# Prefetching streamed K blocks ahead of the output store, and a low-rank FFN loop skewed by five instead of four

## The reference, cut to what matters

```python
x = L0_attn_x                                   # (4, 8192, 1024) float32
q = x @ Wq;  k = x @ Wk;  v = x @ Wv            # 1024 x 1024 each
s = q @ k^T, causal, scaled by 1/32
x = layernorm(x + softmax(s) @ v @ Wo)
P = x @ U1                                      # 1024 -> 256
H = gelu(P @ V1 + b1)                           # 256 -> 4096
Q = H @ U2                                      # 4096 -> 256
x = layernorm(x + Q @ V2 + b2)                  # 256 -> 1024
```

## Time and profile before

| | us |
|---|---|
| median of 2 runs | 2522.15 (2521.6 to 2522.7) |
| profiled execution, its own time | 2539.7 |
| its span, slowest core (core 6) | 2538.2 |
| spans of its 8 cores | 2498.4 to 2538.2 |
| mean granted TensorE clock of its cores | 0.938 to 0.944 |

### The profile page before, as it was taken

How to read it: one execution, slowest core, us unless ns; L and a number is a source line. 1 busy time by engine, 2 the same in 40 slices (tenths; PEclk the granted TensorE clock), 3 DMA queues, 4 the chain that set the end, 5 groups by cost and what they waited for, 6 DMA issues and landing times.

```text
span 2538.2 us, 43250 instructions; the slowest of 8 cores (2498.4 to 2538.2 us)
## 1 busy us (share of the span) xinstructions
PE 2166.1 (85%) x14288; PEld 1353.6 (53%) x14288; DVE 770.8 (30%) x1882; ACT 665.7 (26%) x1389; POOL 353.0 (14%) x653
## 2 busy tenths in 40 slices
PE   0799899999677798788898989898979799897995
PEld 0354445555345465556565556565656566565663
DVE  0233334444235533432314141404040311303104
ACT  0000000000034344424334242424243332423323
POOL 3001111111310010110110202030202112021120
PEclk9999899999878898899898989898989899898997
DMA  9979998886361121132241616171717356182560
GB/s 125 143 99 150 142 135 164 168 163 146 104 105 42 55 84 46 59 134 82 85 152 49 216 49 218 67 233 37 255 59 257 110 171 220 59 293 82 184 223 17
DMA packets 219886, 328.79 MB, mean 130 GB/s; under 512 B 122688, under 2 KB 127824, under 8 KB 218656
## 3 DMA queue, kind: packets, MB, share of 16 engines
q0 software_dynamic: 51120, 166.84, 27.3%
q1 hardware_dynamic: 168560, 159.18, 23.2%
HBM read 287.92 MB, written 77.07 MB: 144 GB/s over the span
## 4 chain that ended last, share of the span: by engine, by line
PE 54%; DVE 7%; ACT 4%; issue 3%; DVEq 3%; POOL 1%; DMA 1%; ACTq 0%; POOLq 0%; SPq 0%
PE ps_s L499 16%; PE ps_a L524 9%; PE ps_a L526 8%; PE ps_x L614 5%; PE ps_a L627 4%; PE ps_a L565 2%; PE ps_s L565 2%; DVE x1t L782 1%; PE ps_s L627 1%; DVEq L807 1%; PE ps_a L499 1%; PE ps_x L549 1%; PE ps_s L646 1%; PE ps_s L549 1%; DVE x L808 1%
## 5 line engine op out<-in xcount | busy, mean ns | idle before, releaser
L663 ACT ACTIVATE p_sb<-ps_s,shift_s 128x256 bf16<-128x256 f32 x512 | 240.8, 473 | 696.1 <-PE ps_s L499 696.0
L499 PE MATMUL ps_s<-qg,kst 128*128 128x256 bf16 x2808 | 363.3, 272 | 3.6 <-DMA kst<-kscr 3.6
L403 POOL DMA_DIRECT2D vst<-vscr x351 | 188.0, 538 | 1131.7 <-PE ps_a L526 1045.6
L499 PEld LDWEIGHTS ps_s<-qg,kst 128*128 128x128 bf16 x2808 | 272.7, 97 | 112.3 <-issue 5.2
L252 PE MATMUL ps_s<-xt,wk_sb 128*128 128x512 bf16 x1024 | 228.9, 384 | 79.9 <-DMA wk_sb<-wk 50.1
L526 PE MATMUL ps_a<-vst,p_sb 128*128 128x512 bf16 x702 | 264.7, 377 | 0.0
L524 PE MATMUL ps_a<-vst,p_sb 128*128 128x512 bf16 x702 | 264.0, 376 | 0.0
L750 DVE RECIPROCAL recip<-ps_x 128x1 f32<-128x1 f32 x32 | 3.7, 158 | 771.4 <-PE ps_a L526 771.2
L663 ACT ACT_TABLE_LOAD x30 | 38.5, 1283 | 694.0 <-PE ps_a L499 693.8
L627 PE MATMUL ps_a<-p_sb,v_sb 128*128 128x256 bf16 x704 | 146.9, 310 | 85.2 <-DVE p_sb L824 85.2
L522 PE MATMUL ps_x<-ones_b,p_sb 128*128 128x1 bf16 x1088 | 180.4, 166 | 36.2 <-POOL p_sb L409 28.0
(11 more groups left out here) (109 smaller groups left out, 2517.5 us busy)
## 6 DMA issues: line engine op xcount, KB each, us to landing
vst<-vscr POOLq DMA_DIRECT2D x351, 256.0 KB, 4.6
kst<-kscr SPq DMA_DIRECT2D x351, 256.0 KB, 4.7
xbf<-x_seq POOLq DMA_DIRECT2D x16, 1024.0 KB, 14.6
xo<-x_own SPq DMA_DIRECT2D x32, 512.0 KB, 4.2
out<-outb SPq DMA_DIRECT2D x32, 512.0 KB, 3.2
kscr<-kstage POOLq DMA_DIRECT2D x51, 256.0 KB, 7.0
vscr<-vstage POOLq DMA_DIRECT2D x51, 256.0 KB, 3.5
xobf<-x_own POOLq DMA_DIRECT2D x16, 512.0 KB, 17.9
```

Of the source, the lines that this page charges most:

```text
L403: g.dma_start(out=vst[:, slot * 1024:(slot + 1) * 1024], in_=vscr_a[kb - R]).then_inc(vstS[slot], 16)
L499: mm = t.matmul(sbank(kb), k_tile(g_i, kb, dc), qg[:, qb + dc * 256:qb + (dc + 1) * 256], start=(dc == 0), stop=(dc == 7))
L663: sc.activation(p_sb[:, (it % 3) * 256:(it % 3 + 1) * 256], sbank(kb), AF.Exp, bias=shift_s[:, 0:1], scale=SCALE).then_inc(sem_exp, 1)
```

## The change

It has two parts. In SP's queue, `out_dma(g_i - 1)` moves from before the K loads of group `g_i` to behind them. In the FFN loop, `q2_partial` runs five slices behind `h` and no longer four, so that TensorE's order is h(0) to h(5), q2(0), h(6), q2(1), ..., h(31), q2(26), then q2(27) to q2(31). No instruction is added or dropped, and no wait is changed.

```diff
                 for g_i in range(NG):
-                    if g_i > 0:
-                        out_dma(g_i - 1)
                     for kb in range(R, 4 * g_i + 4):
                         si = SI[(g_i, kb)]
                         if si >= RING:
@@
                         slot = si % RING
                         s.dma_start(out=kst[:, slot * 1024:(slot + 1) * 1024],
                                     in_=kscr_a[kb - R]).then_inc(kstS[slot], 16)
+                    if g_i > 0:
+                        out_dma(g_i - 1)
                     gg = g_i + 2
@@
                         mm.then_inc(sem_h, 1)
-                        if fc >= 4:
-                            q2_partial(fc - 4)
-                    for fc in range(28, 32):
+                        if fc >= 5:
+                            q2_partial(fc - 5)
+                    for fc in range(27, 32):
                         q2_partial(fc)
```

## The result

| | before | after |
|---|---|---|
| median, us | 2534.67 (13 runs) | 2510.66 (14 runs) |
| ratio after / before, comparable runs | | 0.9933 (95%: 0.9906 to 0.9959) |
| profiled execution, span of the slowest core | 2538.2 | 2513.2 |
| the same, mean over 8 cores | 2513.0 | 2496.8 |
| first scores of phase 2 (L499) to the end, mean (range) over cores | 1848.5 (1845.0 to 1852.4) | 1832.2 (1830.8 to 1833.5) |

The medians hold disturbed runs too, so the ratio, made without them, is the number to go by. The change makes the kernel 0.67% faster (0.41 to 0.94%), about 17 us; the forecast was 5 us. Phase 1 is untouched but differs by up to 35 us between cores and runs (650.5 to 685.7 us over all profiled executions), so from here on phase 2 is compared, in the mean of the eight cores of one profiled execution of each kernel. There the gain of 16.3 us stands clear of the spread between cores.

A forecast was written before the change was run, and what follows sets the result against it. TensorE, busy 85% of the span, was taken to bound the kernel, so only its gaps could be won. Against the median: 2522.15 - 3.4 (skew) - 1.8 (K loads) = 2517 us, range 2511 to 2525.

The forecast's parts named there:

- Direction, and that no more than 2% is at stake: Whole kernel: faster, at 2517 us, with a change of less than 2% (50 us) given chance 0.985.
- Their sum, 10.1 us, is close to all that can be won: TensorE's waits: 6.5 us for the first GELUs plus 3.6 us for K blocks, 0.4% of the time.
- The gap: FFN loop start: h(5) ahead of q2(0) fills 0.43 of 0.61 us empty; q2(0) starts when it did.
- I therefore hold the moment fixed: FFN loop after restart: the clock's rise stays put, so 0.43 us of low-clock work saves 0.21 us behind it.
- 16 x 0.21 = 3.4 us: Skew's gain over 16 FFN loops: 0.21 us each, 3.4 us in total.
- The sign that I gave for being right: FFN loops in the changed profile: low-clock stretches after a restart keep their range of 3.7 to 6.2 us.
- the rise moves with the work: FFN loop: the clock rises earlier with the moved work, skew worth 6.9 us, time 2513.5 us; chance 0.15.
- Does the loop give it back at its end?: FFN loop end: ScalarE and the h_sb ring can follow, so nothing of the skew's gain is given back.
- 0.08 us to spare: FFN loop end before the change: GELU(31) ends at 2035.90, q2(31) issues at about 2035.98.
- The K loads: SP's queue: K loads ahead of the store remove TensorE's K waits, 3.6 us on core 6, 1.8 against the median.
- The slower rival: Late store delays a group's last blocks if landing passes 14.3 us; 3.6 us excess in 11 groups costs 40; chance 0.03.
- Nothing to be seen: Low-clock stretches shift by chance, about 2.4 us, and the slowest core has no K wait: 2520 to 2524; chance 0.26.

The follow-up runs named there:

- filled gap: Kernel before, with the two matmuls of h(5) run once extra after h(4), in TensorE's idle time, result overwritten; ratio 0.9948 (0.9921 to 0.9975).
- K loads first: Kernel before, with only the K loads moved ahead of the store and the skew still four; ratio 1.0006 (0.9987 to 1.0025).
- half filled: Kernel before, with one extra matmul of 256 columns after h(4) instead of two; ratio 0.9996 (0.9974 to 1.0018).
- early table: Kernel before, with a one-column GELU after the square root of L699, so ScalarE loads its table earlier; ratio 0.9952 (0.9933 to 0.9972).
- 256 columns: Kernel before, with K loads ahead of the store, skew four, and an extra GELU of 256 columns ahead of the first; timed once, 2537.2 us.

## Why the prediction was right or wrong

- **Direction, and that no more than 2% is at stake: right. The size: too small.** 17 us were won where 5 stood. The range, 2511 to 2525, reached to 11 us faster, and only the end of the interval (0.9959, which is 2512 us) touches it. That the median after, 2510.66, looks close to 2511 is luck, since the median before it was 2534.67 and not 2522.15.
- **"Their sum, 10.1 us, is close to all that can be won": failed.** Both waits are gone, as forecast, but phase 2 became 16.3 us shorter. The list of waits shows idle time; what an idle stretch costs later through the clock doesn't stand in it.
- **The gap: right.** 0.43 of 0.61 us filled, q2(0) 2.69 us after the restart in both kernels.
- **"I therefore hold the moment fixed": this step failed**, and with it the size (5 us forecast, 17 measured). It is the term "16 x 0.21 = 3.4 us" of the sum. The three lengths of the earlier trace rows, 6.18, 3.74 and 5.68 us, were read as showing that the rise does not depend on what TensorE does. They show only that the same sequence meets the rise at different distances. They can't show what another sequence would do, and all three loops had the same gap. The filled gap (4.15 us a loop against 5.12, with no work moved) shows that the distances become shorter on average. The sign that I gave for being right, low-clock stretches that keep their range of 3.7 to 6.2 us, did not come: on core 6 they ran from 3.9 to 6.4 us before and from 2.8 to 5.8 after. The term of the sum that was mis-sized is the skew's: 3.4 us forecast, 12.8 measured, of which 8.5 are the earlier rise (16.9 us of low-clock time, halved) and 3.4 the term as it was worked out; the other 0.9 us is at the end of the loop (below).
- **The rival "the rise moves with the work" was also too small.** It allowed 0.43 us a loop, 6.9 us in all; the rise came 1.06 us earlier on average. The upper bound of this term was no bound. (The Trainium skill, "TensorE: Matmul & The Clock Gate", "What's actually happening", which I weighed for its budget of time, names the recent busyness of the array as what sets the clock. The filled gap agrees with that, 4.15 against 5.12 us at the same order of the work; I took the one sentence for the whole rule.)
- **"Does the loop give it back at its end?" No, and it gained 2.9 us, a term that I had put at nothing.** I counted 0.08 us to spare for q2(31) and no cost. Group 12 of core 6 after, with the earlier trace rows to hold against it, and below it q2(31) by itself, before and after:

```profile
1995.91 0.91 ACT L706 ACTIVATE h_sb<-ps_a,b_sb 128x256 bf16<-128x256 f32 x2
1995.92 1.30 PEld L614 LDWEIGHTS ps_x<-h_sb,u_sb 128*128 128x128 bf16 x12
1996.03 1.47 PE L614 MATMUL ps_x<-h_sb,u_sb 128*128 128x256 bf16 x12
...
1997.34 1.91 PE L499 MATMUL ps_a<-qg,kres 128*128 128x256 bf16 x16
```

```profile
2036.04 0.38 PE L614 MATMUL ps_x<-h_sb,u_sb 128*128 128x256 bf16 x2
```

```profile
1997.12 0.38 PE L614 MATMUL ps_x<-h_sb,u_sb 128*128 128x256 bf16 x2
```

  Before, GELU(31) ended at 2035.90 and q2(31) started at 2036.04, not at my 2035.98. The 0.08 us to spare left out the time from the end of a GELU to the start of the matmul that waits for it. With the old skew that is 0.14 us in all 128 loops, in each of the kernels (before, K loads first, gap filled, half filled, early table, 256 columns), and q2(31) starts about 0.17 us behind the matmul ahead of it; with the new skew it is 0.11. That is 0.06 us a loop, 1.0 in 16, the 0.9 us that were missing above. Behind the loop the scores follow 0.11 us after the last start, where it was 0.23: in the 15 loops that scores follow, this step took 3.7 us in total in each of the six kernels with the old skew, and 1.8 in each of the four with the new one and no extra matmuls. So both parts belong to the skew. The first is the wait for GELU(31); why the second goes with it no run took apart.
- **The K loads: right in mechanism, at the top end in size.** The wait is gone on all cores, the loads follow the x tiles, the late store disturbs nobody. I put 3.6 us on core 6 and 1.8 against the median; the steps from a V product to the scores show 0.2 to 1.3 in the mean of the cores, and the whole shows nothing (1.0006, 0.9987 to 1.0025). The slower rival did not happen: V and K loads land in at most 7.1 and 7.8 us, far from 14.3.
- **"Nothing to be seen"** rested on low-clock stretches shifting with chance signs. Single loops do shift both ways (94 of 128 down, 34 up), but the mean of 16 went down on each of the eight cores, by 0.7 to 1.3 us a loop. The chance is in the single loop, and the gap moves the mean.

## What to carry to other kernels

Where TensorE restarts at the lower clock, a short gap soon after the restart can cost more than its own length: here 0.61 us cost 0.3 us of work and another 0.5 us by the later rise, per loop and on average. When such a gap is costed, don't hold the moment of the rise fixed; bound it by what a version without a gap could reach, and look first for what makes the gap (here a table load of 1.28 us that fits into ScalarE's idle time ahead). A wait in front of a restart that can't be removed can be filled with matmuls nobody reads, if they are sized to end with the wait: 18 of them took the loops from 254 to 243 us, and 24 with the table loaded early took them to 223 us. And when an engine's result is counted as just in time, add the time from its end to the start of what waits for it, 0.14 us here.

## What the runs showed of the hardware

- A gap just after the restart has a graded effect on the mean low-clock stretch, 4.15 to 6.68 us a loop for 0.18 to 0.90 us, and less behind more matmuls (0.47 us behind twelve had none).
- Matmuls whose result is overwritten or never read bring the clock up like any others: 66.3 us of low-clock time with the extra pair, 64.6 with the useful one.
- A store of 512 KB, one of two placed among the last loads of a group, takes 6.1 us to land instead of 3.2 (medians of 32).
- In all 14 profiled executions the granted clock has two levels only, 0.5 and 1.0, with matmuls on all eight cores.
- Removing low-clock time where TensorE's pace is not the limit gives almost nothing: 29 us less of it outside the loops made that stretch 1.2 us shorter.
